# Layer 0's softmax scale on the queries, and other orders for the lists of the bridge

## The reference, cut to what matters

```python
def _L0_xattn_ref(latents, context, Wq, Wk, Wv, Wo):       # H=16 heads, KV=4 groups, HD=96
    hidden = jnp.concatenate([context, latents], axis=1)
    q = (latents @ Wq.T)...; k = (hidden @ Wk.T)...; v = (hidden @ Wv.T)...
    scale = 1.0 / jnp.sqrt(jnp.asarray(HD, q.dtype))
    scores = jnp.einsum('bkgqd,bksd->bkgqs', q, k) * scale
    attn = jax.nn.softmax(scores.astype(jnp.float32), axis=-1).astype(q.dtype)
    out = jnp.einsum('bkgqs,bksd->bkgqd', attn, v)
    return out.reshape(...) @ Wo.T
x = x + tanh(g_xattn[0]) * _L0_xattn_ref(_layernorm(x), ctx, ...)
x = x + tanh(g_ffn[0])   * _L0_ffn_ref(_layernorm(x), ...)      # base product + 8 experts of rank 8, top 2
x = x + tanh(g_xattn[1]) * _L1_xattn_ref(_layernorm(x), ctx, ctx) # linear attention
x = x + tanh(g_ffn[1])   * _L1_ffn_ref(_layernorm(x), ...)      # base product + Fourier-coded update
x = x + tanh(g_xattn[2]) * _L2_xattn_ref(...)                   # 32 heads of 128, rotary embedding
```

## Time and profile before

| | |
|---|---|
| median of 3 runs | 1714.86 us (1713.06 to 1717.67) |
| profiled execution, own time | 1716.31 us |
| its span | 1714.4 us |
| TensorE busy | 1686.2 us, 98% |
| VectorE, ScalarE, GpSimd busy | 1291.4 us (75%), 872.3 us (51%), 973.8 us (57%) |
| mean granted TensorE clock | 0.999 |
| bridge, about | 300 to 490 us |

### The profile page before, as it was taken

How to read it: one execution, slowest core, us unless ns; L and a number is a source line. 1 busy time by engine, 2 the same in 40 slices (tenths; PEclk the granted TensorE clock), 3 DMA queues, 4 the chain that set the end, 5 groups by cost and what they waited for, 6 DMA issues and landing times.

```text
span 1714.4 us, 27528 instructions
## 1 busy us (share of the span) xinstructions
PE 1686.2 (98%) x8808; PEld 1417.0 (83%) x8808; DVE 1291.4 (75%) x2378; ACT 872.3 (51%) x2435; POOL 973.8 (57%) x808
## 2 busy tenths in 40 slices
PE   7999999999999999999999999999999999999999
PEld 6888888776878888888888888888888888888887
DVE  6576666788887777777787788787777877777796
ACT  7666575654554545445354453454543545445451
POOL 3223232466585757657576574575665757657662
PEclk9999999999999999999999999999999999999999
DMA  6001010030110101101021111110110101101101
GB/s 212 25 26 38 13 32 11 23 106 7 56 50 25 49 14 60 37 24 43 18 61 37 31 42 32 32 54 22 47 37 24 49 21 53 37 24 49 37 13 50
DMA packets 37428, 69.45 MB, mean 41 GB/s; under 512 B 4426, under 2 KB 5194, under 8 KB 37234
## 3 DMA queue, kind: packets, MB, share of 16 engines
q1 hardware_dynamic: 37362, 68.61, 13.3%
HBM read 66.50 MB, written 2.10 MB: 40 GB/s over the span
## 4 chain that ended last, share of the span: by engine, by line
PE 90%; DVE 4%; issue 2%; POOL 2%; ACT 2%; DMA 0%; SPq 0%; DVEq 0%; ACTq 0%; POOLq 0%
PE ps L445 25%; PE ps L447 25%; PE ps L446 25%; PE ps L715 4%; PE ps L692 4%; PE ps L693 2%; PE ps L624 1%; PE ps L655 1%; ACT probs L2665 1%; PE ps L961 1%; POOL probs L3463 1%; POOL rope_a L3445 1%; DVE rope_b L1570 1%; DVE rope_b L1571 0%; PE ps L962 0%
## 5 line engine op out<-in xcount | busy, mean ns | idle before, releaser
L3463 POOL TENSOR_TENSOR probs<-probs,rsums 128x512 f32<-128x512 f32 (+1 forms) x160 | 195.0, 1218 | 256.3 <-DVE rsums L1606 255.2
L3445 POOL TENSOR_TENSOR rope_a<-rope_a,rope_b 128x512 f32<-128x512 f32 x160 | 207.0, 1294 | 220.4 <-DVE rope_b L1571 220.2
L2665 ACT ACTIVATE probs<-probs,negmax 128x128 f32<-128x128 f32 x512 | 200.9, 398 | 97.9 <-DVE negmax L1580 97.8
L445 PE MATMUL ps<-wo_hiL,ot_hi 128*128 128x512 f32 x608 | 244.6, 402 | 4.8 <-DVE ot_lo L1621 3.5
L445 PE MATMUL ps<-xt_hi,wq_hiL 128*128 128x512 f32 x608 | 243.3, 400 | 0.3 <-DVE xt_lo L1506 0.2
L447 PE MATMUL ps<-wo_hiL,ot_lo 128*128 128x512 f32 x608 | 238.4, 392 | 0.0
L447 PE MATMUL ps<-xt_hi,wq_loL 128*128 128x512 f32 x608 | 237.7, 391 | 0.0
L446 PE MATMUL ps<-wo_loL,ot_hi 128*128 128x512 f32 x608 | 237.6, 391 | 0.0
L446 PE MATMUL ps<-xt_lo,wq_hiL 128*128 128x512 f32 x608 | 236.7, 389 | 0.0
L2681 ACT CAST ot_hi<-ps 128x512 fp32r<-128x512 f32 (+1 forms) x160 | 90.4, 565 | 213.5 <-PE ps L447 212.1
L2674 ACT CAST pt_hiL<-ps 128x512 fp32r<-128x512 f32 (+1 forms) x160 | 107.8, 674 | 167.1 <-PE ps L715 108.3
(11 more groups left out here) (231 smaller groups left out, 4308.3 us busy)
## 6 DMA issues: line engine op xcount, KB each, us to landing
raw<-in_L_proj SPq DMA_DIRECT2D x108, 256.0 KB, 2.7
raw<-in_L_out SPq DMA_DIRECT2D x76, 256.0 KB, 2.8
raw<-in_F_w SPq DMA_DIRECT2D x16, 256.0 KB, 2.7
ct_raw<-in_ctx_t SPq DMA_DIRECT2D x8, 256.0 KB, 6.2
x<-in_x SPq DMA_DIRECT2D x8, 256.0 KB, 6.2
cn_raw<-in_ctx SPq DMA_DIRECT2D x8, 256.0 KB, 7.3
out<-x SPq DMA_DIRECT2D x8, 256.0 KB, 2.1
raw<-in_L_kv SPq DMA_DIRECT2D x6, 256.0 KB, 3.0
```

The source lines that it names most:

```text
L445: pe.matmul(dst, l_hi, r_hi, start=start, stop=False)
L2665: e = act.activation(probs[:, row:row + L.keys], src, ACT.Exp, bias=offset[:, b % 2, h:h + 1], scale=L.scale, accum_out=sums[:, b % 2, h:h ...
L3445: gp.tensor_tensor(rope_a[:, a], rope_a[:, a], rope_b[:], ALU.add).then_inc(L.s_rsum, 1)
L3463: gp.tensor_tensor(pv, pv, rsums[:, b % 2].unsqueeze(2).to_broadcast([P, GH, L.keys]), ALU.mult).then_inc(L.s_p, 1)
```

## The change

The scale is applied to the queries as they are evicted: ScalarE writes scale x value into the high part, and VectorE computes scale x value minus the high part. So the scores come out scaled, the maximum is the bias as it stands, exps(b) waits for row_max and carries no scale, and the step on L1588, its tile and its semaphore are gone. Besides, the four lists of the bridge get another order. The same entries stand in each. The core of the diff (of the lists, the stretches of which the prediction speaks; in other places entries swap with near neighbours in the same manner):

```diff
@@ VectorE, evacuate: query tile of layer 0
-v.tensor_tensor(L.q_lo[0:hd, n, tok], ps[0:hd, bank, :], L.q_hi[0:hd, n, tok], ALU.subtract)
+v.scalar_tensor_tensor(out=L.q_lo[0:hd, n, tok], in0=ps[0:hd, bank, :], scalar=L.scale,
+                       in1=L.q_hi[0:hd, n, tok], op0=ALU.mult, op1=ALU.subtract)
...
@@ VectorE, row_max
                     v.tensor_reduce(negmax[:, b % 2], sc, X_AXIS, ALU.max, negate=True).then_inc(L.s_smax, 1)
-                    v.wait_ge(L.s_smax, B * i + b + 1)
-                    v.tensor_scalar(nbias[:, b % 2], negmax[:, b % 2], L.scale, None, ALU.mult).then_inc(L.s_nb, 1)
@@ ScalarE, head and exps
-                        act.copy(L.q_hi[0:hd, n, tok], ps[0:hd, bank, :])
+                        act.mul(L.q_hi[0:hd, n, tok], ps[0:hd, bank, :], L.scale)
...
-                                           bias=offset[:, b % 2, h:h + 1], scale=L.scale,
+                                           bias=negmax[:, b % 2, h:h + 1],
@@ TensorE, bridge
                 a0.scores(5, last)
+                a0.transposes(4, last)
                 pe.wait_ge(Lq[0].s_qk, Lq[0].ready("KQ", last, 1))
                 pe.wait_ge(Lq[0].s_v, Lq[0].ready("V", last, 1))
                 norm_transpose("F0", 0)
-                a0.transposes(4, last)
...
+                a0.transposes(6, last)
                 norm_transpose("F0", 2)
-                a0.transposes(6, last)
...
                 numerators(7)
+                pe.wait_ge(a_rec, 2)
+                a2.begin(3, 0)
                 norm_transpose("F1", 4)
                 products(1, 3)
                 norm_transpose("F1", 5)
                 products(1, 4)
+                norm_transpose("F1", 6)
                 products(1, 5)
-                norm_transpose("F1", 6)
-                pe.wait_ge(a_rec, 2)
-                a2.begin(3, 0)
@@ VectorE, bridge
                 a0.pt_tail(2, last)
                 a0.evacuate(2, 0, last)
+                a0.row_sum(3, last)
+                norm_rows("F0", 0)
                 a0.residual(1, last)
-                a0.row_sum(3, last)
                 a0.next_stats(1, last)
                 a0.ot_tail(2, last)
...
                 a0.pt_tail(5, last)
+                norm_tail("F0", 0)
+                a0.row_sum(6, last)
                 a0.residual(4, last)
+                a0.next_stats(4, last)
+                a0.ot_tail(5, last)
+                a0.row_max(7, last)
                 norm_rows("F0", 3)
-                a0.row_sum(6, last)
-                a0.next_stats(4, last)
-                norm_tail("F0", 0)
-                a0.row_max(7, last)
-                a0.ot_tail(5, last)
                 a0.pt_tail(6, last)
@@ ScalarE, bridge
                 a0.wo_head(0, last)
+                a0.wo_head(1, last)
+                a0.wo_head(2, last)
                 a0.exps(0, last)
...
+                a0.pt_head(2, last)
+                a0.exps(3, last)
+                a0.head(2, 0, last)
+                a0.o_head(2, last)
@@ GpSimd, bridge
                 add_bias(1, 0)
                 add_bias(1, 1)
+                a2.weights(0)
                 norm_rstd("F1", 3)
...
-                add_bias(1, 4)
...
+                kvs_tail()
                 one_hot(2)
-                kvs_tail()
+                one_hot(3)
```

More of the change, by code:

```diff
@@ L1284, in bridge @@
                 a0.out_proj(1, last)
+                a0.fillers(2, last, only=1)
                 a0.heads_out(2, last)
-                a0.fillers(2, last, only=1)
                 a0.scores(4, last)
@@ L1347, in bridge @@
                 experts(0, 7)
+                numerators(0)
                 spread_out(0)
-                numerators(0)
                 l1_weight(3)
@@ L1360, in bridge @@
                 norm_transpose("F1", 0)
+                rope_table(2)
                 numerators(3)
@@ L2275, in bridge @@
                 a0.pt_tail(1, last)
-                a0.residual(0, last)
                 a0.row_sum(2, last)
                 a0.evacuate(1, 0, last)
+                a0.residual(0, last)
+                a0.row_max(3, last)
+                a0.ot_tail(1, last)
+                a0.evacuate(1, 1, last)
                 a0.next_stats(0, last)
[L2280 to L2283, removed]
                 a0.pt_tail(2, last)
                 a0.evacuate(2, 0, last)
+                a0.row_sum(3, last)
+                norm_rows("F0", 0)
                 a0.residual(1, last)
-                a0.row_sum(3, last)
                 a0.next_stats(1, last)
@@ L2293, in bridge @@
                 a0.row_sum(4, last)
-                norm_rows("F0", 1)
+                a0.evacuate(2, 1, last)
                 a0.next_stats(2, last)
-                a0.evacuate(2, 1, last)
                 a0.ot_tail(3, last)
@@ L2299, in bridge @@
                 a0.pt_tail(4, last)
-                a0.residual(3, last)
+                norm_rows("F0", 1)
                 norm_rows("F0", 2)
                 a0.row_sum(5, last)
+                a0.residual(3, last)
                 a0.next_stats(3, last)
@@ L2323, in bridge @@
                 a0.pt_tail(7, last)
+                norm_tail("F0", 2)
                 summed(0, 1)
+                norm_tail("F0", 3)
                 a0.residual(6, last)
-                norm_tail("F0", 3)
                 norm_rows("F0", 5)
                 a0.ot_tail(7, last)
+                a0.next_stats(6, last)
+                summed(0, 2)
                 norm_tail("F0", 4)
-                summed(0, 2)
                 norm_tail("F0", 5)
@@ L2355, in bridge @@
                 logits(0, 1)
+                next_stats("A1", f_x, 1)
                 residual(0, 2)
@@ L2635, in head @@
                         act.wait_ge(L.s_proj, t + 1)
-                        act.copy(L.q_hi[0:hd, n, tok], ps[0:hd, bank, :])
-                        act.copy(L.q_hi[part, GH - 1, tok], ps[hd:P, bank, :]).then_inc(L.s_qk_head, 1)
+                        act.mul(L.q_hi[0:hd, n, tok], ps[0:hd, bank, :], L.scale)
+                        act.mul(L.q_hi[part, GH - 1, tok], ps[hd:P, bank, :], L.scale).then_inc(L.s_qk_head, 1)
                         return
@@ L3270, in bridge @@
                 base_weight(1, 3)
+                spread_copy(3)
+                norm_rows("F1", 1)
+                table_copy(0)
+                table_copy(1)
+                spread_copy(4)
                 act.wait_ge(f_h, B)
@@ L3767, in bridge @@
                 a0.wo_tail(0, last)
+                a0.wo_tail(1, last)
+                a0.wo_tail(2, last)
                 a0.normalise(0, last)
-                a0.wo_tail(1, last)
                 a0.normalise(1, last)
-                a0.wo_tail(2, last)
                 a0.normalise(2, last)
@@ L3774, in bridge @@
                 a0.normalise(3, last)
+                gate_weight(0)
+                a0.normalise(4, last)
+                a0.base_weight(0)
                 norm_rstd("F0", 1)
-                a0.normalise(4, last)
                 norm_rstd("F0", 2)
-                gate_weight(0)
-                a0.base_weight(0)
+                a0.normalise(5, last)
                 a0.base_weight(1)
-                a0.normalise(5, last)
+                norm_rstd("F0", 3)
                 a0.base_weight(2)
                 a0.base_weight(3)
-                norm_rstd("F0", 3)
                 a0.normalise(6, last)
-                expert_weight(0)
                 norm_rstd("F0", 4)
```

285 lines of the change are left out of this document (134 added, 151 removed).

## The result

| | before | after |
|---|---|---|
| median (lowest to highest), 20 runs each | 1714.66 us (1713.06 to 1717.67) | 1719.72 us (1715.35 to 1722.98) |
| ratio, 95% interval | | 1.0025 [1.0019, 1.0032] |
| profiled execution, span, mean granted clock | 1716.31, 1714.4, 0.999 | 1721.51, 1719.7, 0.996 |

The forecast was 1710.8 (1706.5 to 1715.5). The time lies outside the range, and the sign is wrong. The executions of the changed kernel differ by their granted clock: the three at 1.000 took 1715.35 to 1716.51 us, the seven at 0.996 took 1721.39 to 1722.98.

The account below looks back on a forecast made before the run. TensorE, busy 98% of the span, was taken as the bound, with one large hole before out_proj(5). Terms 3.1 + 0.4 + 0 + 0.3 - 0.2 + 0.5 = 4.1 us gave median 1710.8, range 1706.5 to 1715.5.

Parts of the forecast that it names:

- Second half (373 to 500 us): Bridge's second half, TensorE close to gapless: three waits cost about 1 us, half won, 0.5; bounds -1.0 and 2.0.
- second use of the rule: norm_rows(F0, 5), right before ot_tail(7), could stand behind a GpSimd subtraction; by the port-lock rule the sum would be 1.6 smaller.
- norm_rows(F0, 0): Right behind row_sum(3), beside GpSimd's normalisation of batch 3: a hazard of 0 to 0.5 us, 0.2 put in as loss.
- ot_tail(5) before row_max(7): VectorE order swap closing the hole before out_proj(5): 3.9 us off, 0.8 given back, net 3.1; bounds 2.3 and 3.9.
- No scaled bias: 32 steps, 7.1 us, leave VectorE; only 2 of the bridge's 8 count, 0.4 us gained; bounds 0 and 1.6.
- Scale at the query's eviction: Layer 0's query tiles: longer evictions on VectorE and ScalarE, covered by TensorE; cost 0, at most 3 us.
- The other moves in the first half: Bridge's first half, transposes(4), exps(3) and others reordered: +0.3 us gained; bounds -0.5 and 0.8.
- The moved key tile: a2.begin(3, 0) moves from 457.14 to 447.64, taking rope products out of the crowded stretch; part of the second half's 0.5.
- The first query-key product of layer 2: Key sign, behind the query tile of 487.44: it comes 4 us earlier, then the two traces run in parallel.
- A: Larger gain: VectorE's idle stretches in the bridge close too, 6.2 us, median 1708.7; chance 0.20.
- B: No gain: the saved time reappears one step on, at GpSimd's one-hots before rope_table(0); median 1714.6; chance 0.15.
- C: Slower: at a2.begin(3, 0) TensorE waits 4.8 us for GpSimd's low weights, and the clock falls; median 1717.6; chance 0.07.

Follow-up runs that it names:

- e1: Changed kernel with weigh(0, 0) put back ahead of norm_tail(F0, 6) and (7) on VectorE: 1712.98 us, ratio 0.9991.
- e2: Changed kernel with only ScalarE's table_head() moved behind turned(0, 0), so GpSimd's table subtraction starts later: 1712.90 us, ratio 0.9988.
- e7: Changed kernel with products(0, 3) put ahead of turn(0, 0) on TensorE: 1712.62 us, ratio 0.9986.
- e3: Kernel before with weigh(0, 0) moved behind norm_tail(F0, 6) and (7): 1721.82 us, ratio 1.0042.
- e5: Kernel before's code (query copy, scaled bias step) with the changed kernel's four lists: 1730.73 us, ratio 1.0092.
- e13: Code edits with the old lists up to scores(7) and normalise(6); behind, changed lists with weighing early, products(0, 3) ahead, norm_rows(F0, 3) behind pt_tail(6): 1712.74 us.
- e10: Code edits with the kernel before's lists, only ot_tail(5) put ahead of row_max(7) on VectorE: 1712.53 us, ratio 0.9983.
- e4: The changed kernel's code edits (queries scaled at eviction, no bias step) with the kernel before's four lists: 1712.45 us, ratio 0.9989.
- e12: Changed kernel with weighing early, products(0, 3) ahead of turn(0, 0), norm_rows(F0, 3) behind pt_tail(6), next_stats(1) behind pt_tail(3): 1712.24 us, ratio 0.9989.
- e11: Kernel before, unchanged, run again for a second profiled execution: 1715.35 us, ratio 1.0001.

## Why the prediction was wrong, step by step

**The step that failed: "Second half (373 to 500 us)".** The diff moved weigh(0, 0) behind two norm tails, and I followed in that stretch only the key tile of layer 2. I bounded the step by "-1.0 (one new handover)"; the collision with GpSimd's subtraction of 2.37 us made the weighing 3.0 us longer, which is 2.6 us of hole on TensorE, and 4.6 more by the clock. Shown from both sides: e1, e2 and e7 take the loss away in three ways, e3 puts it into the kernel before.

The Trainium skill ("SBUF — State Buffer", Who interferes with whom) has a VectorE instruction with two SBUF inputs contend with a GpSimd instruction that reads SBUF; the port pair that they share it calls an exclusive lock. The traces agree: 0.63 us became 3.66 (after), 3.70 (e7) and 2.68 (e3). In after, e5 and e7 the first two products got through and the third took 2.4 us; in e3, where GpSimd was already at work, the first took 1.40 and the second 1.08. I had this rule in hand, used it for norm_rows and not for `weigh(0, 0)`, whose two inputs lie in SBUF and for which TensorE waits.

The Trainium skill's rule as my prediction has it, that whichever starts second waits for the other's whole instruction, fits these products but not every case. norm_rows(F0, 5) started 0.07 us ahead of GpSimd in e5 by the trace and waited all the same; with a lead of 0.39 (changed kernel) and 0.21 (e13) it came through in 0.59 and 0.54 us. So this second use of the rule named a real hazard, which the changed kernel did not meet.

**norm_rows(F0, 0): the 0.2 is there, but it is not new.** GpSimd's normalisation of batch 3, started 0.16 us into norm_rows, took 2.10 us and not 1.89: 0.2 more, and not the 0.5 that the prediction worked out from the rule. The kernel before pays the same one batch later, where norm_rows(F0, 1) stands right behind row_sum(4): 2.12 us. The new list takes that one away (1.89 at 337.20), so the term should have been 0. The kernel before, then the changed one:

```profile
335.63 0.54 DVE L1492 TENSOR_SCALAR xn<-x,mv,rstd 128x512 f32<-128x512 f32 x1
335.80 2.12 POOL L3463 TENSOR_TENSOR probs<-probs,rsums 128x1024 f32<-128x1024 f32 x1 [3.96 <-DVE rsums L1606]
...
329.90 0.52 DVE L1490 TENSOR_SCALAR xn<-x,mv,rstd 128x512 f32<-128x512 f32 x1
330.06 2.10 POOL L3460 TENSOR_TENSOR probs<-probs,rsums 128x1024 f32<-128x1024 f32 x1 [2.10 <-DVE rsums L1604]
```

**ot_tail(5) before row_max(7): right in the place, wrong in the size.** In the trace it came as written: no hole at out_proj(5), heads_out(6) late by 0.65 (forecast 0.8), no low clock near 350. But of the 3.9 us of that place 1.35 were a clock loss (14.81 against 13.46) that the next execution had elsewhere; it belongs to the executions at 0.999 (8 of the 27 measured beside e1), not to the median. And the 2.4 us do not stay: alone the swap is worth 0.7 (12.77 against 13.46), and nothing once the bias step is gone (e10 against e4: +0.2). I gave back 0.8 at heads_out(6), and did not follow row_max(7) down its own chain: maximum, exps, sum, normalise, transposes(7).

**No scaled bias: 1.9 us and not 0.4**, beyond my bound of 1.6 (1407.05 against 1410.46 less the 1.5 of lower clock at 308). Of it 1.07 are at out_proj(5): the bias step there was the one that took 1.07 us, so two of my terms share one hole. It gave 0.3 in heads_out(0) to heads_out(5), and 0.2 at scores(1). The remaining 0.3 stand behind the bridge, where the bias step has no part; the traces with the old code differ there by 0.24 among themselves (1220.22 to 1220.46), so this bit is not shown to be its work.

**Scale at the query's eviction: cost 0, right.** e4's first group of the bridge starts at 299.69 us of its span, the kernel before's at 300.37 and 300.46. ScalarE's multiplying eviction takes 592 ns against 582, near the lower of my bounds (0.58 and 0.82) and not at my 0.68. VectorE's takes 694 ns against 693; my 0.06 more for the kind was wrong.

```profile
L2635 ACT ACTIVATE q_hiL<-ps 32x512 fp32r<-32x512 f32 x24 | 14.2, 592 | 0.3
...
L1551 DVE SCALAR_TENSOR_TENSOR q_loL<-ps,q_hiL 32x512 fp32r<-32x512 f32 x24 | 16.6, 694 | 0.3
```

**The other moves in the first half** cost 0.6 us (37.24 against 36.67) where I wrote +0.3. e12 moved one entry away from ot_tail(2) and has 37.01 in that stretch: part of the cause, not all. **The moved key tile** gained nothing: 95.69 against 95.58, for the forecast +0.5. The first query-key product of layer 2, which should have come 4 us earlier, came 5.7 later (495.99 against 490.26).

Taken together the list moves other than the weighing are worth zero: e1 and e7 have 1407.2 to 1407.3, e4 1407.05. My forecast gave them 3.7 of its 4.1 us (3.1 + 0.3 - 0.2 + 0.5). The rivals: A, a larger gain, had nothing for it. B, "the saved time reappears one step on", was right for the lists, with the chain of a batch in the place of the one-hots. C had the right kind (one new wait, and the clock behind it) at the wrong place: wkv_lo was never waited for there.

Open: why the product behind the blocked one takes 1.08 us (GpSimd's next instruction had started 0.04 us before it, but lasts 3.63), what lead over GpSimd is enough, and what decides whether a hole of 2.5 us is followed by the lower clock.

## What to carry to other kernels

When the order of a hand-written list changes, go through every VectorE entry with two SBUF inputs or a plain tensor-scalar form that TensorE waits for, and lay it against GpSimd's long instructions: a margin of a few tenths of a microsecond, 0.6 in the kernel before, is not one. Where such a wait cannot be kept apart, cover it on TensorE with work that is ready, as e7 does with one line. And before a term counts a stretch at the lower clock, look at more than one execution of the same kernel: it may stand elsewhere in the next.

## What the runs showed of the hardware

- Four equal VectorE products, 0.22 us each when alone, took 0.21, 0.22, 2.38 and 1.08 us: the third started just after GpSimd's subtraction (after; the same in e5 and e7).
- A blocked VectorE instruction may wait for more than one of GpSimd's: 0.54 us became 3.92 behind two in a row (e5), and the two GpSimd instructions were as long as ever (1.27, 2.33).
- The hole at out_proj(5) was followed by a stretch at the lower clock in one execution of the kernel before (2.46 us, clock 0.59 in 355 to 357), and by the full clock in the other (2.46, e11) and in e3 (2.45). Behind the hole at `turn(0,0)`, of 2.3 to 2.5 us, the clock was at the lower level for some ten microseconds in all three profiles that had it (after, e3, e5), and the mean clock was 0.998 or less in 17 of 20 executions of the changed kernel. TensorE ran short matmuls behind that hole and long ones behind the other; whether this matters was not tried.
- Behind smaller holes at 305 to 308 us (0.84 and 0.49 in e7, 1.04 and 0.49 in e11) the clock sometimes falls and sometimes not: the kernel before took 5.88 us from scores(1) to heads_out(0) in one execution and 7.39 in the other.
